# A fused attention and feed-forward block on one core: the transfers of the rows of maxima are issued by ScalarE instead of the sync queue

## What is computed

```python
scores = jnp.einsum('bhtd,bhsd->bhts', q, k) * scale + bias[None]
scores = jnp.where(causal[None, None], scores, -jnp.inf)
w = jax.nn.softmax(scores, axis=-1)
out = jnp.einsum('bhts,bhsd->bhtd', w, v)        # then @ Wp + bp, layer norm, + x
out = r * einsum(square(relu(k)), W_v)           # feed-forward, then layer norm, + x
```

## Time and profile before

| what | value |
|---|---|
| time, median of 3 runs | 2242.05 us (2239.59 to 2242.39) |
| time of the profiled execution | 2240.61 us |
| span of the profiled execution | 2238.8 us |
| PE / DVE / ACT / POOL busy, share of the span | 94% / 87% / 75% / 75% |
| granted TensorE clock, mean | 0.987 of full speed |
| shift_all<-shift_row transfers | 256, of 1.0 KB each |

### The profile page before, as it was taken

One profiled execution on the slowest core, in us unless ns is written; L12 is line 12 of the kernel. 1 busy time (PEld: TensorE's weight loads), 2 busy tenths in 40 slices (PEclk: granted clock), 3 DMA queues, 4 the chain that ended last, 5 costly groups with the idle time before them and its releaser, 6 DMA issues. The chain is left out here.

```text
span 2238.8 us, 74837 instructions
## 1 busy us (share of the span) xinstructions
PE 2110.4 (94%) x29456; PEld 1431.2 (64%) x29456; DVE 1945.4 (87%) x5209; ACT 1686.2 (75%) x2526; POOL 1682.9 (75%) x1370
## 2 busy tenths in 40 slices
PE   2798889999999999999999999999999999999975
PEld 1355556666666667666666766666676667667664
DVE  6777778998999989998999999999999988888856
ACT  2578788877877877887778778777877877887733
POOL 1367677887888888888888888888888887777851
PEclk9899999999999999999999999999999999999998
DMA  7111112222222222332222233223222322221260
GB/s 175 34 45 49 45 42 66 61 61 71 73 62 68 69 64 61 71 72 62 68 69 65 61 70 73 64 67 69 63 61 71 73 59 66 57 55 52 70 124 22
DMA packets 336783, 147.11 MB, mean 66 GB/s; under 512 B 172976, under 2 KB 335664, under 8 KB 336432
## 3 DMA queue, kind: packets, MB, share of 16 engines
q1 hardware_dynamic: 336432, 142.33, 26.6%
HBM read 24.25 MB, written 43.06 MB: 30 GB/s over the span
## 5 line engine op out<-in xcount | busy, mean ns | idle before, releaser
L1657 POOL TENSOR_TENSOR probs<-probs_f,probs 128x1024 f16<-128x1024 f32 (+3 forms) x704 | 1121.8, 1604 | 351.2 <-ACT probs L951 348.6
L933 ACT ACTIVATE probs_f<-score_ps,score_unit 128x1024 f32<-128x1024 f32 (+3 forms) x704 | 621.2, 882 | 239.1 <-DVE score_ps L1216 113.4
L1200 DVE TENSOR_REDUCE row_max<-max_ps 128x2 f32<-128x1024 f32 (+2 forms) x640 | 632.0, 1004 | 18.6 <-PE max_ps L644 15.8
L951 ACT CAST probs<-probs_f 128x1024 f16<-128x1024 f32 (+3 forms) x704 | 566.8, 814 | 12.3
L678 PEld LDWEIGHTS misc<-v_pair,probs 128*128 128x128 f16 x4608 | 414.6, 97 | 39.7 <-issue 28.8
L678 PE MATMUL misc<-v_pair,probs 128*128 128x65 f16 x4608 | 437.7, 194 | 0.6 <-issue 0.6
L679 PE MATMUL misc<-v_pair,probs 128*128 128x64 f16 x4608 | 436.1, 193 | 0.0
L680 PE MATMUL misc<-v_pair,probs 128*128 128x65 f16 x4608 | 435.1, 193 | 0.0
L680 PEld LDWEIGHTS misc<-v_pair,probs 128*128 128x128 f16 x4608 | 417.6, 97 | 0.0
L679 PEld LDWEIGHTS misc<-v_pair,probs 128*128 128x128 f16 x4608 | 417.5, 97 | 0.0
L569 PE MATMUL misc<-xT,w_split 128*128 128x512 f16 x1536 | 370.1, 384 | 21.7 <-issue 9.4
(11 more groups left out here) (168 smaller groups left out, 3634.9 us busy)
## 6 DMA issues: line engine op xcount, KB each, us to landing
v_pair<-v_calc SPq DMA_DIRECT2D x64, 516.0 KB, 3.6
o_scratch<-o_stage SPq DMA_DIRECT2D x128, 256.0 KB, 2.4
xh<-x SPq DMA_DIRECT2D x56, 128.0 KB, 2.1
x_res<-x SPq DMA_DIRECT2D x56, 128.0 KB, 3.1
out<-out_sb SPq DMA_DIRECT2D x56, 128.0 KB, 1.7
shift_all<-shift_row SPq DMA_DIRECT2D x256, 1.0 KB
probs<-wqkv SPq DMA_DIRECT2D x1, 3072.0 KB, 13.9
probs<-band_scratch SPq DMA_DIRECT2D x8, 144.0 KB, 3.8
```

The source lines that it names most:

```text
L933: nc.scalar.activation(dst, score_ps[t % 2][:, :, 0:width], ACT.Exp, scale=score_unit[:]).then_inc(exp_done, 1)
L951: nc.scalar.copy(dst, src).then_inc(hi_done, 1)
L1200: last = dve.tensor_reduce(dst[:, :, i % 4:i % 4 + 1], max_ps[:, :, col:col + width], AX.X, ALU.max)
L1657: pool.tensor_tensor(low, copy_of(par + ahead, t)[:, 0:2 * width], high, ALU.subtract).then_inc(lo_done_pool, 1)
```

## The change

`load_shift` moves from SP's program into ACT's. It waits for the semaphore of the row (`shift_ready[c]`), passes the same empty instruction, and issues the same two transfers. In ACT's body it stands right behind the `shift` that makes the row, for both halves; in SP's body both calls are gone. For c = 1 this is also another body: SP issued them at the start of the next body, ACT does at the end of this one.

```diff
@@ SP
-            def load_shift(m, par, ahead, c):
-
-                side, _ = parity(m, par, ahead)
-                held(shift_ready[c], 2 * m + par + ahead + 1)
-                for h in range(2):
-                    sp.dma_start(shift_all[side][D * h:D * h + 1, c * 512:(c + 1) * 512],
-                                 shift_row[c][4 * h:4 * h + 4, :]).then_inc(shift_in[c][side], 16)
...
-                    if has["att"]:
-                        load_shift(m, par, 0, 1)
...
-                    if has["next"]:
-                        load_shift(m, par, 1, 0)
@@ ACT
+            def load_shift(m, par, ahead, c):
+
+                side, _ = parity(m, par, ahead)
+                act.wait_ge(shift_ready[c], 2 * m + par + ahead + 1)
+                plain(act)
+                for h in range(2):
+                    act.dma_start(shift_all[side][D * h:D * h + 1, c * 512:(c + 1) * 512],
+                                  shift_row[c][4 * h:4 * h + 4, :]).then_inc(shift_in[c][side], 16)
...
                     if has["next"]:
                         shift(m, par, 1, 0)
+                        load_shift(m, par, 1, 0)
                     if has["qkv"]:
                         high_part("q1", m, par, at)
...
                     if has["next"]:
                         shift(m, par, 1, 1)
+                        load_shift(m, par, 1, 1)
                     if has["mix"]:
                         tail_gate(n)
```

## The result

The changed kernel takes 2334.98 us (median of 4 runs, 2333.88 to 2335.97) against 2241.36 us (2239.59 to 2242.39): a ratio of 1.042, 95% interval 1.040 to 1.0436, slower by 94 us. The forecast was 2330 us, its range 2270 to 2370.

A forecast was written before the change was run, and what follows sets the result against it. PE's own stream was taken to set the pace. 52 later bodies at 1.54 us plus ten early ones at 1.34, less 4.3, gave +89 us on 2240.61: 2330 us, range 2270 to 2370.

The forecast's parts named there:

- d: Delay of what stands behind the row and its two issues on ACT: 1.47 us, bounds 0.95 and 1.81.
- Place A: ACT's row of c = 0, ahead of q1's cast: PE loses 1.02 us per later body plus ACT's lateness on arrival.
- the slack of 0.45 us: Room between DVE's low part of q1 and PE's weigh_values(1): 0.49 less 0.04 us.
- the term for the signal: Time a signal takes from the end of DVE's low part of q1 to PE's start: 0.04 us.
- The chain cast, low part, bank: ACT's q1 cast, then DVE's low part, which gives PE bank 0 back: only 0.45 us of slack.
- Place B: ACT's row of c = 1, ahead of tile 0's work: PE 0.35 us late, ACT 0.52 us late afterwards.
- the gain: PE's waits for transfers into shift_all saved by earlier landing: -4.3 us booked, bound -10.9 us.
- The early bodies: First ten bodies, without later stages: only the c = 0 row costs, 1.34 us each, 13.4 us in all.
- rival 1: ACT's idle time absorbs the issues and earlier landing pays: 2236 us, down to 2230; chance 0.11.
- rival 2: Issues on ACT are short, at the lower price of SP's 128 KB transfers: 2271 us; chance 0.17.
- rival 3: ACT's issue waits while SP's transposing load is issued, once per body: up to 2480 us; chance 0.04.
- Rival 4: Same path costs more: DVE does not win back lateness, ACT dispatches slower after issues: 2340 to 2370 us; chance 0.13.

The follow-up runs named there:

- experiment 2: Kernel before, plus ACT waiting for its own row and passing the empty instruction at both places, all transfers still on SP: 2242.52 us, ratio 1.0012.
- experiment 3: Changed kernel with one issue per row on ACT (the other on SP), 2271.57 us, or with a third issue added on ACT, 2423.46 us.
- c0_later: Changed kernel with the issues of c = 0 put behind q1's cast on ACT: 2264.39 us, ratio 1.0107.
- sp_early: Kernel before, all issues on SP, those of c = 1 moved into the body that makes their row, ahead of store_out and transpose_head: 2235.02 us, ratio 0.998.
- only_c0: Kernel before with only the transfers of c = 0 moved to ACT, c = 1 staying on SP: 2315.85 us, ratio 1.034.
- both_later: Changed kernel with ACT's issues of c = 0 behind q1's cast and those of c = 1 at the body's end: 2236.04 us, ratio 0.9987.
- only_c1: Kernel before with only the transfers of c = 1 moved to ACT, c = 0 staying on SP: 2264.66 us, ratio 1.0116.
- one_each: Changed kernel with head 0's transfer of each row issued by ACT and head 1's by SP: 2271.57 us, ratio 1.0145.

## Why the prediction was right, step by step

- **The cost of an issue on ACT.** Taken from SP's rows at 1.20 us for two; measured 1.19 to 1.21. d was put at 1.47 us and is 1.40 at A, 1.48 at B. That the wait itself is small (0.2 us) is shown by experiment 2, that each issue adds 0.6 us to d by experiment 3. By the Trainium skill (Perfetto Trace Analysis, DMA Instruction, HWDGE) the sequencer is free for its next instruction where the profiled time of an issue ends; here the trace agrees, with 0.04 to 0.10 us between them.
- **Place A.** Forecast: DVE idle about 1.5 us, PE 1.0 to 1.3. Measured: 1.48, and 1.06 us of lateness. d less the slack of 0.45 us would have been 0.95. The difference is the term for the signal: I had taken 0.04 us from the end of DVE's low part to PE's start, and once PE really waits for it, it is 0.15 us (1074.28 to 1074.43; computed from the timelines, the same in all 47 such waits between 400 and 2000 us, while it is 0.06 us before the score of tile 2). So the slack was 0.34 us, and 1.40 - 0.34 = 1.06. The chain cast, low part, bank is shown by `c0_later`, which takes away nothing but the order of issue and cast and loses the whole cost of A.
- **Place B.** Put at 0.35 us on PE, with 0.52 us of lateness on ACT carried into A. Measured: 0.43 us at the score of tile 2 and 0.10 us at q0, which I had not followed: DVE's lateness reaches PE a second time through bank 0. The lateness carried into A is no larger than PE's own. So a body costs 0.52 + 1.07 = 1.59 us, not 0.52 + 1.47 - 0.45 = 1.54. That the sum came out so close is in part luck: d at A was 0.07 us smaller and the slack 0.11 us smaller than I had them, and the two nearly cancel.
- **The total.** Forecast for the 52 later bodies +80.1 us before the gain, measured +74.0 with it. A regular body went from 32.34 to 33.92 us (1055.75 to 1089.67), +1.58; 52 of them would be +82 us. `sp_early`, which changes nothing but when the row of c = 1 lands, takes 1692.4 us for the same 52 bodies (390.18 to 2082.53) where the kernel before takes 1698.2 (389.68 to 2087.91): the gain is 5.9 us, where I had booked 4.3 from the 4.3 and 6.6 us of waits in the earlier trace rows. That leaves 2 us, and body 14 holds them. It is one of the bodies (14, 22, 30, 38, 46, 54) in which q0 takes the x of a new batch and PE waits for the transposed x. It lasts 36.14 us before (519.44 to 555.58), 36.40 in `sp_early` and 35.21 with the change. In the kernel before, PE waits 2.28 us for the transposed x and then runs 3.4 us at half the clock; with the change the wait is 1.33 us and the clock stays at 1.00. Why the clock fell in one and not in the other is not shown (`only_c0` waited 2.4 us there and kept its clock), so these 2 us are not shown to come of the change. The other 51 bodies are 1.59 us longer each than in `sp_early`. Body 14 before and with the change:

```profile
519.44:555.58 36.14, 33.86 (x462) 22.76 (x462) 30.38 (x87) 26.00 (x39) 26.84 (x23) 0.95 0.27 61
544.12:579.33 35.21, 32.52 (x462) 22.24 (x462) 30.50 (x87) 26.08 (x39) 26.83 (x23) 1.00 0.29 63
```

- **The early bodies.** Forecast +13.4, measured +14.3.
- **What I had not booked**: 4.5 us before body 0. 1.1 us of it came before any row was made: the first transposition of maxima stands at 65.95 us before and at 67.04 with the change, and between 65.8 and 68.0 in the ten kernels, which run the same work up to there. In body -1 the two issues took 1.79 us (see below) and DVE stood 3.1 us before its first q_lo, where it had stood 1.0, which is another 2 us. The rest stays open.
- **Rivals.** ACT's idle time did not take it (rival 1): 1.40 + 1.48 = 2.9 us of it were asked for, less than the 6.6 us that there are, but where there is none. `both_later` gives rival 1's time, 2236 us, once the issues stand elsewhere. Issues were not short (rival 2). SP's transposing load moved to 1063.80, 8 us ahead of the issues of c = 0, and met no issue of ACT in the whole execution (rival 3); where issues of the two queues did run side by side, they hardly got in each other's way (see the last section). Rival 4, the same path at 2340 us or more, did not come: DVE won back what it was to win back, and B cost 0.52 us as in the sum.

## What to carry to other kernels

Before an issue is moved to an engine that computes, price it at what the sync queue pays for the same transfer and look at what stands behind it in that engine's order, down to who waits for that; the engine's idle share did not tell it here. If it must stand there, put it behind the instruction on the chain and not directly behind its producer: here one instruction further for c = 0, and six for c = 1, made 4.2% into nothing. When a transfer starts late, first look at the order of the queue that has it; here moving it up in SP's own order won as much as any kernel did, 3.6 us.

## What the runs showed of the hardware

- An issue on ACT's queue took 580 ns at least and 581 in the median, 1174 at most, where SP's took 572, 588 and 770:

```profile
L912 ACTq DMA_DIRECT2D shift_all<-shift_row x256: 580/581/1174, 67.8 to 2213.0; - x128
```

- The long one is the first issue on ACT's queue: 1174 ns at 67.8 us, the next longest 778. With the second it makes the 1.79 us in body -1. In all seven kernels in which ACT issues, its first issue took 1163 to 1178 ns, in `only_c1` too, where it stands at 81.5 us. Why is open.
- Issues of the two queues can run side by side. In `one_each` both engines issue at place A within 0.06 us of each other in 63 of 64 bodies; there ACT's issues took 581 ns in the median and SP's 597, where SP's at this place took 581 in the kernel before (computed from the timelines). One issue of ACT fell beside a transposing load of SP's (2.53 us) and took 592 ns. The two rows over all of `one_each`:

```profile
L402 SPq DMA_DIRECT2D shift_all<-shift_row x128: 572/618/768, 67.8 to 2155.6; - x128
L924 ACTq DMA_DIRECT2D shift_all<-shift_row x128: 580/581/1178, 67.8 to 2151.1; - x128
```

- An issue overlaps with instructions that ACT had begun or been given before it: in `both_later` 1.21 us of issuing at the end of the body made exponential 1 only 0.23 us later. Directly behind a wait for the running instruction nothing is left to overlap with, and the full 1.40 and 1.48 us are paid at A and B.
